# Sums of squared activations moved from VectorE to GpSimd in a fused macaron layer

## The reference

```python
x = x + 0.5 * ffn(layernorm(x))      # first feed-forward layer
x = x + attn(layernorm(x))           # 16 heads of width 8, rotary, softmax over all 2048 tokens
x = x + 0.5 * ffn(layernorm(x))      # second feed-forward layer

def ffn(x):                          # W_fc 512 x 128, W_proj 128 x 512, both made ternary
    h = gelu(x @ ternary(W_fc).T)    # 2048 x 512
    h = layernorm(h, ln_w, ln_b)     # over the 512 hidden values of a token
    return h @ ternary(W_proj).T
```

## Time and profile before

| | us |
|---|---|
| median of 3 runs | 752.54 |
| lowest and highest | 752.45 and 753.93 |
| the profiled execution, its own time | 753.2 |
| its span, first to last instruction | 751.4 |
| busy in the span: TensorE, VectorE | 722.7, 690.1 |
| busy in the span: ScalarE, GpSimd | 628.6, 277.6 |

### The profile page before, as it was taken

How to read it: one execution, slowest core, us unless ns; L and a number is a source line. 1 busy time by engine, 2 the same in 40 slices (tenths; PEclk the granted TensorE clock), 3 DMA queues, 4 the chain that set the end, 5 groups by cost and what they waited for, 6 DMA issues and landing times.

```text
span 751.4 us, 17517 instructions
## 1 busy us (share of the span) xinstructions
PE 722.7 (96%) x6801; PEld 238.8 (32%) x6801; DVE 690.1 (92%) x876; ACT 628.6 (84%) x1190; POOL 277.6 (37%) x560
## 2 busy tenths in 40 slices
PE   5998989999999999999999999999999999999994
PEld 2763321222222222222222222222222222224383
DVE  6898899999999999999999999999999999996374
ACT  3554434999999999999999999999999999999842
POOL 4536334455454552333222222232233232424221
PEclk8997875999999999999999999999999999999998
DMA  7003110000011011110000000000000000000001
GB/s 225 5 1 78 34 48 1 5 5 25 14 26 36 18 23 33 23 34 13 4 4 4 4 5 4 20 3 5 3 5 4 5 7 20 8 6 5 6 15 42
DMA packets 25247, 15.51 MB, mean 21 GB/s; under 512 B 14134, under 2 KB 23158, under 8 KB 24902
## 3 DMA queue, kind: packets, MB, share of 16 engines
q1 hardware_dynamic: 12940, 10.84, 5.3%
q0 software_dynamic: 10016, 3.02, 2.2%
q10 hardware_dynamic: 2208, 0.53, 0.4%
HBM read 9.41 MB, written 3.31 MB: 17 GB/s over the span
## 4 chain that ended last, share of the span: by engine, by line
PE 80%; DVE 14%; issue 2%; ACT 1%; POOL 1%; DMA 1%; POOLq 0%; DVEq 0%; SPq 0%; ACTq 0%
PE ps L1388 33%; PE ps L1373 20%; PE ps L1352 13%; DVE mh L891 12%; PE ps L1228 4%; PE ps L1286 3%; PE ps L1303 2%; PE ps L1293 1%; PE ps L1324 1%; PE ps L1239 1%; PE ps L1403 1%; DMA X<-in_L_attn_x_dram 1%; PE ps L1217 1%; PE ps L1312 1%; PE ps L1413 0%
## 5 line engine op out<-in xcount | busy, mean ns | idle before, releaser
L891 DVE TENSOR_REDUCE mh<-ps 128x2 f32<-128x1024 f32 x512 | 586.6, 1212 | 10.5 <-PE ps L1352 9.9
L1185 ACT ACTIVATE ring<-ps 128x512 f32<-128x512 f32 x1024 | 550.3, 600 | 31.6 <-PE ps L1373 17.4
L1388 PE MATMUL ps<-ring,Vx 128*32 128x256 f32 x4096 | 325.8, 392 | 0.9 <-ACT outT L1193 0.9
L1373 PE MATMUL ps<-QT,KT 51*128 51x512 bf16 x1024 | 214.6, 389 | 1.1
L1352 PE MATMUL ps<-KT,QT 48*128 48x512 bf16 x1024 | 209.0, 389 | 2.7 <-ACT QT L1106 1.6
L1388 PEld LDWEIGHTS ps<-ring,Vx 128*32 128x32 f32 x4096 | 82.3, 108 | 187.2 <-ACT ring L1185 166.9
L1373 PEld LDWEIGHTS ps<-QT,KT 51*128 51x128 bf16 x1024 | 52.8, 93 | 220.2 <-ACT ring L1185 205.5
L630 POOL DMA_DIRECT2D rope<-outT x80 | 43.0, 542 | 185.8 <-ACT outT L1193 177.8
L619 POOL DMA_DIRECT2D QT<-mrow x128 | 71.3, 562 | 42.1 <-DVE mrow L908 37.5
L1352 PEld LDWEIGHTS ps<-KT,QT 48*128 48x128 bf16 x1024 | 50.6, 95 | 32.7 <-issue 14.3
L607 POOL TENSOR_TENSOR mp<-zeros,top 128x8 bf16<-128x8 f32 x32 | 6.4, 200 | 140.9 <-DVE top L899 140.8
(11 more groups left out here) (136 smaller groups left out, 371.1 us busy)
## 6 DMA issues: line engine op xcount, KB each, us to landing
rope<-rope_tables SPq DMA_DIRECT2D x2, 1024.0 KB, 6.7
QT<-mrow SPq DMA_DIRECT2D x128, 0.8 KB
QT<-mrow POOLq DMA_DIRECT2D x128, 0.8 KB, 1.7
rope<-outT POOLq DMA_DIRECT2D x80, 8.0 KB, 1.7
rope<-outT SPq DMA_DIRECT2D x80, 8.0 KB
q_bounce<-XB SPq DMA_DIRECT2D x3, 384.0 KB, 2.8
QT<-q_bounce SPq DMA_DIRECT2D x18, 64.0 KB
QT<-q_bounce POOLq DMA_DIRECT2D x18, 64.0 KB, 3.3
```

The source lines that it names most:

```text
L891: v.tensor_reduce(mh[:, g % 2, :, q, kb], ps[:, bank:bank + 2, :], AX.X, ALU.max)\
L1185: a.activation(ring[:, n % PRING, :], ps[:, exp_bank(n), :], ACT.Exp, scale=SCALE).then_inc(p_ready, 1)
L1373: t.matmul(ps[:, exp_bank(n), :], KT[rows, j, kt * P:(kt + 1) * P], QT[rows, j, c * CS:(c + 1) * CS], start=True, stop=True).then_inc(b_re ...
L1388: mm = t.matmul(ps[r:r + 32, PO, 0:QH], Vx[:, kt, col:col + 32], ring[:, (2 * n + h) % PRING, half * QH:(half + 1) * QH], start=(kt == 0), ...
```

## The change

The three additions of add_squares(0) to add_squares(3) go from VectorE to GpSimd. There each addition waits for its own input block (s_ready) and for the addition before it (a new semaphore, sq_step), where VectorE drained its pipeline between them. The residual sums of chunks 2 and 3 now stand behind add_squares(0). The additions of the second feed-forward layer (chunks 4 to 7) stay on VectorE.

```diff
             pool.wait_ge(wbar_ready, 2)
-            for c in range(NC):
-                residual(0, c)
+            residual(0, 0)
+            residual(0, 1)
+            def add_squares(n):
+
+                pool.wait_ge(s_ready, n * KH + 2)
+                if n >= 2:
+                    pool.wait_ge(pr_ready, n - 1)
+                to = sqsum[:, n % 2, :]
+                g.tensor_tensor(to, sq[:, 0, :], sq[:, 1, :], ALU.add).then_inc(sq_step, 1)
+                pool.wait_ge(s_ready, n * KH + 3)
+                pool.wait_ge(sq_step, 2 * n + 1)
+                g.tensor_tensor(to, to, sq[:, 2, :], ALU.add).then_inc(sq_step, 1)
+                pool.wait_ge(s_ready, n * KH + 4)
+                pool.wait_ge(sq_step, 2 * n + 2)
+                g.tensor_tensor(to, to, sq[:, 3, :], ALU.add).then_inc(sq_ready, 1)
+
+            add_squares(0)
+            residual(0, 2)
+            residual(0, 3)
             hidden_scale(0, 0)
+            add_squares(1)
             ln_scale(1, 0, 0)
             hidden_scale(0, 1)
             ln_scale(1, 1, 1)
+            add_squares(2)
             hidden_scale(0, 2)
             ln_scale(1, 2, 2)
+            add_squares(3)
             hidden_scale(0, 3)
             ln_scale(1, 3, 3)
...
             norm_rows(0, X, 2, 2)
             row_stats(X, 3, 3)
-            add_squares(0)
             norm_rows(0, X, 3, 3)
             variance(0)
-            add_squares(1)
             update(0)
...
             turned_half("K0", 0)
             turned_half("K0", 1)
-            add_squares(2)
             norm1(1)
...
             turned_sum("Q0")
-            add_squares(3)
             rest("Q0")
```

More of the change, by code:

```diff
@@ L249, in macaron @@
         sq_ready = sem("sq_ready")
+        sq_step = sem("sq_step")
         hid_used = sem("hid_used")
```

## The result

The changed kernel took 761.37 us (median of 4 runs, 759.27 to 762.49) against 752.5 for the kernel before in the same comparison: ratio 1.012, 95% interval 1.009 to 1.015. That is 8.9 us slower. The profiled execution took 762.13, with a span of 760.3, against 753.2 and 751.4. The forecast was 759.4 in a range of 756.5 to 763.0.

What follows compares the result with a forecast made beforehand. TensorE's own program order was taken as the bound; four waits of 1.9, 1.9, 0.2 and 2.9 sum to 6.9 us. Added to the profiled 753.2 that gives 760.1, less 0.7 for the median 759.4; range 756.5 to 763.0.

Steps and rivals of the forecast that it cites:

- a granted clock of 0.50 between 24 and 66 us: Sign of being wrong: TensorE's clock at half rate in that stretch, where it was granted 1.00 from 24 to 60.
- The removal bought nothing: Taking 12 additions, 8.8 us, off VectorE in the first feed-forward layer was costed at nothing, hidden by TensorE's 99% share.
- The rival in which VectorE was the bound: VectorE the true bound from 24 to 66.6 us: its relief gives back at most 2.6 us, so 750; chance 0.03.
- An addition on GpSimd takes 1.28 us: Each 128x512 f32 addition takes 1.28 us plus 0.08 gap, so a chunk's sum takes 4.0 us against 2.2.
- First wait 1.9: At sum_squares of the first chunk: TensorE arrives at 31.23, GpSimd's sums run to 33.1, 1.9 us late.
- Second wait 1.9: At sum_squares of the second chunk: GpSimd's sum ends at 40.8, TensorE arrives at 38.9, 1.9 us more.
- Third wait 0.2: At the third sum_squares: GpSimd's sum, behind ln_scale(1,1,1), ends at 51.3, TensorE arrives at 51.1, 0.2 us more.
- Fourth wait 2.9: At the fourth sum_squares: GpSimd's sum, behind ln_scale(1,2,2), ends at 63.9, TensorE arrives at 61.0, 2.9 us more.
- Sum 6.9: TensorE's four waits for GpSimd's sums, 1.9 + 1.9 + 0.2 + 2.9 = 6.9 us, absorbed by nothing later; chance 0.65.
- Mutual blocking: Rival: every VectorE instruction meeting a GpSimd sum also delays it, 3.6 us instead of 0.3, so 762.7; chance 0.10.
- The clock falls in a pause: Rival: TensorE's clock falls to half rate in its new pauses, costing 1.7 to 3.4 us, 761.1 to 762.8; chance 0.14.
- Half rate given back: Rival: TensorE does the half-rate stretch from 66.6 us at full rate, returning up to 6.8: 752.6 to 757; chance 0.06.

Runs made afterwards that it cites:

- one addition of three: Changed kernel with only the first of three additions per first-layer chunk, leaving out two of four blocks: 750.47 us against 751.22 before, ratio 0.9985.
- alone: Four kernels, each with only one first-layer chunk's sum on GpSimd, the others on VectorE: chunk 0 755.96, chunk 1 754.84, chunk 2 752.64, chunk 3 757.04 us.
- four filled pauses: Changed kernel with 8, 8, 3 and 11 dummy matmuls ahead of the four sum_squares: 760.13 us against 751.23 before, ratio 1.0106.
- the repeat: Changed kernel measured once more without edit, which also gave its second trace: 760.83 us against 751.22 before, ratio 1.0123.
- split kernel: Kernel before, whole computation, with GpSimd making the first of three additions per first-layer chunk and VectorE the other two: 753.07 us against 752.45, ratio 1.0023.
- two additions: Changed kernel with two of three additions per first-layer chunk, leaving out one of four blocks: 755.64 us against 751.23 before, ratio 1.0057.
- two pauses filled: Changed kernel with 8 dummy matmuls ahead of sum_squares(0) and 11 ahead of sum_squares(3): 759.66 us against 751.22 before, ratio 1.0094.
- sums first: Changed kernel with add_squares(0) ahead of all residual sums on GpSimd, residual sums 2 and 3 behind ln_scale(1,0,0): 764.02 us against 751.22 before, ratio 1.0149.

## Why the prediction was right

The direction, the four waits and their cause held. Not all of its signs did: sum_squares started at 33.4, 41.5, 52.9 and 65.7 us, where it had 33, 41, 51 and 64; the later stages were not simply 7 us later (the row maximum came at 80.18 us, not near 75.3); and a granted clock of 0.50 between 24 and 66 us, which it had named as a sign of being wrong, did occur. By its own steps:

**The removal bought nothing.** Right. In the changed kernel VectorE waits for TensorE's result ahead of each variance (3.7, 2.6, 0.6 and 4.5 us), and where the sums were in time (one addition of three), the relief gave no measurable gain. The rival in which VectorE was the bound wanted up to 2.6 us up to 66.6 us. The interval of that kernel (0.9958 to 1.0012) would allow it, but its trace does not: TensorE's four sums come 0.0 to 0.1 us earlier than before and the row maximum 0.2 later.

**An addition on GpSimd takes 1.28 us.** Right: 1.26 to 1.33 us, but for two of the fourth sum. The step between two was 0.14, not 0.08: read from small operations, it did not carry over to large ones. The estimate of 1.11 us from the Trainium skill (GPSIMD Engine Reference, section Elementwise — side-by-side cycle accounting) is not what this chip showed; the measurement decides.

**First wait 1.9.** 2.2 measured, alone and together with the others. The longer step makes 0.1 of the difference. The rest, 0.2, is a reading: the prediction took TensorE's arrival from the chain, 31.23, which counts sum_squares from the end of the matmul before it. In the timeline of the kernel before it starts at 31.07:

```profile
31.07 0.95 PE L1293 MATMUL ps<-ones,ring 128*128 128x1 f32 x8
```

**Second wait 1.9.** 2.4 in the changed kernel, 1.7 alone. The changed kernel has something the other has not: residual sums 2 and 3 run while variance(0) is made, and its msq took 1.03 us instead of 0.16 (34.77 to 35.80):

```profile
34.77 1.03 DVE L810 TENSOR_TENSOR msq<-mean 128x4 f32<-128x4 f32 x1
```

Hidden_scale(0,0) starts at 36.36, 0.6 after the residual sums end. I had taken 0.2 for this.

**Third wait 0.2.** 1.1 measured, 1.2 alone. This is the term that was mis-sized most, by 0.9. From one sum_squares to the end of the next sum it took 11.4 us, against 10.5 in the prediction: the result comes 1.1 us after sum_squares starts, not 0.8 (again read from the start on the chain), update waits 0.2 for hidden_scale, and the additions take 4.2.

**Fourth wait 2.9.** 3.1 measured, 3.0 alone. The additions beside VectorE's rest("Q0") and last_part("K0") took 1.39 and 1.52 us: 4.5 for the sum, where the prediction had 4.3.

**Sum 6.9.** 8.7 at the fourth sum, reproduced to 0.04 us by the kernel with four filled pauses, in which the clock was 1.00. The forecast of 759.4 was 2.0 us low, and 1.8 of that are the waits: all four were taken too small, by 0.3, 0.5, 0.9 and 0.2. That the total fits so closely is partly luck: in the profiled execution the clock took 2.9 us and gave 2.9 back, which the sum of waits does not contain, and the repeat measured a loss of 9.6 us.

**Mutual blocking (0.10).** Not the way the changed kernel lost most of its time: by an estimate from the rows above about 1.0 of the 8.7 us, 0.6 at the second sum (msq) and 0.4 at the fourth, where the rival had 3.6. But it is real: the prediction read from the earlier trace rows that GpSimd is hardly delayed, and this held only for the rows it looked at. One of four 128x128 tensor_scalars delays GpSimd by next to nothing. A 128x512 addition of VectorE lengthened a GpSimd instruction by 0.44 us in the split kernel, twice, and by 0.11 and 0.26 at the changed kernel's fourth sum. In all four cases VectorE's had begun first. Where GpSimd's began first (51.49, turned_sum("K0") from 51.61), it took only 0.05 longer, and VectorE's waited. The Trainium skill (Advanced Engine Details and Errata, section Mode Summary) has GpSimd instructions and VectorE instructions in a two-port mode block each other, and lists no such mode for tensor_tensor. The trace agrees that both are held up, but has it for tensor_tensor additions too (1.75 us instead of 0.68), and there the measurement decides.

**The clock falls in a pause (0.14).** It did fall, twice in each of the two traces of the changed kernel, so the event was far likelier than I gave it, and the dense matmuls around the pauses were no protection. Its cost was judged wrong too: behind the first pause it is free, since GpSimd is the bound there; behind the second it cost 0.6 in the second trace; behind the fourth it costs 2.6 to 2.9 us up to the row maximum, and in the two traces 2.9 and 5.1 come back. From the row maximum to the exponentials the kernel before took 51.4 us at a mean granted clock of 0.73, the changed kernel 48.5 at 0.82, the kernel with one addition 46.6 at 0.90:

```profile
68.40:119.80 51.40, 48.10 (x172) 13.53 (x172) 45.51 (x47) 16.80 (x22) 21.56 (x41) 0.73 0.17 43
```

the changed kernel:

```profile
80.20:128.70 48.50, 44.03 (x174) 12.97 (x172) 45.07 (x47) 16.64 (x22) 21.54 (x41) 0.82 0.17 46
```

**Half rate given back (0.06).** Something of the kind happened, 2.9 us in the profiled execution and 5.1 in the second one, and in the first it balanced the fall ahead of it. Whether the shift itself causes it or each execution draws it anew stays open: the kernel with one addition, which shifts nothing, had 4.8 us of it in its trace. The traces are of executions with different mean clocks, 0.967 for the kernel before and 0.983 for the one with one addition, and of the 31 runs of the kernel before one has 0.983 as well.

## What to carry to other kernels

Before work is moved to an idle engine, ask for the time at which its result is needed and for the queue it will stand in. GpSimd was busy 43% of the stretch and still too late four times, since each sum took 1.9 us longer there and stood behind steps that only start when TensorE has given its last result; a late sum then delays the next one. And two engines that run side by side are not independent of each other: a four-element instruction of VectorE took up to 1.15 us instead of 0.16 beside a large one of GpSimd.

## What was not expected of the hardware

- TensorE's clock went from 1.00 to 0.50 behind most pauses of 1.4 to 2.8 us between dense matmuls (changed kernel, two additions, chunks 0 and 3 alone, two pauses filled, sums first, split), but not behind the 1.5 and 1.1 us of chunks 1 and 2 alone, and not behind the first pause, 2.0 us, in the second trace of the changed kernel. The length of the pause alone does not decide it. The 31 runs of the unchanged kernel spread from 747.9 to 754.9 us together with their mean clock.
- A VectorE tensor_tensor on 128x4 elements took 1.03 to 1.15 us beside a residual sum on GpSimd, 0.16 alone. The same arithmetic beside GpSimd's four-element powers was not delayed (0.16 us at 38.36 in the kernel before, beside L511 at 38.20).
- Two VectorE additions and four GpSimd additions, run side by side, took 3.42 and 5.85 us; the two take 1.46 without a residual sum beside them, the four 4.95 beside VectorE's normalisation alone.
- A semaphore step between two dependent GpSimd operations was 0.14 us behind an operation of 1.28, and 0.08 behind one of 0.20.
